# Depthwise convolution of a state-space layer: from ten VectorE taps and six TensorE taps behind a gated recurrence to sixteen taps in 32x32 TensorE tiles that begin inside it

## The chip, the cores and the metric

One NeuronCore of a Trainium2 chip runs the whole program. The metric is the device time of one execution in microseconds (us), the median of several. PE is TensorE, DVE is VectorE, ACT is ScalarE, POOL is GpSimd, SP is SyncE, which here only issues DMAs. DVE, ACT, POOL and SP take their instructions strictly in the order of the program, so a wait at the head of a queue holds everything behind it.

## The reference

The input x has 32 sequences (batches) of 128 time steps with 128 features. The program computes a two-layer model; only its start is touched here:

- a gated recurrence over the 128 time steps, all 32 batches at once: `z = sigmoid(x W_z + h U_z + v_z)`, `r = sigmoid(x W_r + h U_r + v_r)`, `hh = tanh(x W + (r*h) U + v)`, `h = (1-z) h + z hh`. The states of all steps are its output G;
- a state-space layer on G: `zxbcdt = G @ W_in` gives a gate z (256 columns), xBC (384 channels) and dt (8 heads). xBC goes through a causal depthwise convolution of 16 taps along time with a bias, then `silu`. Of its 384 channels 256 are xs (8 heads of 32), 64 are B and 64 are C. The scan `h = h*exp(dt*A) + dt*x*B`, `y = h*C` runs over time for each batch and head; then `y + D*xs`, times `silu(z)`, a root-mean-square norm, `@ W_out`, `y/sqrt(1+y*y)`, `@ W_nl`, and the residual sums.

Behind it follow a local attention, a mixture of experts, two LSTMs, an attention with relative bias and a second mixture. The change doesn't touch those.

## The kernel before

**Order of the work.** Every engine has one hand-written program. `weave(...)` runs several Python generators side by side, one turn (`yield`) each in rotation, and so fixes the order of an engine's queue; semaphores (`inc`, `at`) do the rest. The stages that matter are: the load of x; the recurrence `gru_*` with `mprep_*` (preparation of the state-space weights) woven in; then `mdt_*` (dt and the decay exponents), two workers `mamba_*(wk)` and `conv_*`, all woven; then `cprep_*` (the preparation of the next attention) behind worker 0, while worker 1 ends.

**The recurrence.** Helper `mmh` multiplies a 128x128 weight by a 128x32 state as four matmuls into four column tiles of 32 output rows; a fp32 matmul shows as two LDWEIGHTS and two MATMUL records. A step is: matmuls `gzh` x (U_r, U_z), `tanh` into `gth` on ACT, `grh` and `gq` on DVE, matmul `grh` x U, matmuls `gq` x `gn` for the next step, `tanh` into `ghh`, `gzh` on DVE, and again. PE has a hole while ACT and DVE make `grh` (the first hole) and another while they make `ghh` and `gzh` (the second). Between them go the input projections of later steps (`gru_inputs_pe`, records `X,gw`) in the first hole, and dummy bf16 matmuls that keep PE busy (`gru_warm_pe`, records `identb`). POOL writes each state into G. Banks 0 to 7 of PSUM hold the sums of two groups of 8 steps.

**The convolution.** It starts when the recurrence has ended. The 32 batches are 8 units of 4. For each unit and each of three groups of 128 channels (24 pieces, count n): PE multiplies `win` by G into bank 6; ACT copies it into a padded buffer `XP`; PE adds up the first `NT = 6` taps in bank 7 with diagonal matrices `tap` (128x128 by 512 columns); ACT takes them out with the bias (`B,cb`); DVE adds the other ten taps, each one `scalar_tensor_tensor` of 128x512 (records `work<-work,cw`); ACT and DVE make `silu` from a `tanh` (`conv_act`, `conv_dve`). The C channels are moved to partitions 0 to 63 (the 64x512 records of DVE).

**The scan.** Each worker takes every second unit, 4 units in all, and in each unit one batch after the other (n = 0 to 15). Per batch: ACT makes the decays E (8 heads, records `catt<-tri,catt`), PE sums them with `low` into B1 and B2 (two matmuls of 512 columns), ACT takes `Exp`; PE makes the gate, B^T C and the transposes of xs (`cross`); DVE makes `cbm`, `xdt` (L1007), the product `E*cbm` (L1012); PE makes y in `B0` (D*xs by diagonal `dg`, initial state by `h0T`, 64 records of 128x32 for the heads); DVE finishes y (L1020, L1023, L1024) and the gate. At a unit's end come the norm, transposes, `wout`, a square root and a `reciprocal` of 128x512 (L1040), `wnl`, the sum into X on DVE and X+G on POOL (L1054). Worker 1 starts 14 turns behind worker 0 (`MAMBA_UNIT_TURNS`, 22 against 8).

Of the kernel before, what the change touches and what calls it, by code (L numbers as in the profile page):

```python
# [138 lines left out]
NT = 6  # L139
COND2_LAG = 22  # L140
MAMBA_DT_TURNS = 6
MAMBA_UNIT_TURNS = ((8, 1, 1, 1), (22, 1, 1, 1))
# [20 lines left out]
class Kernel:  # L163
    def __init__(self, nc, ctx, I, out):
# [7 lines left out]
        with nc.sbuf_tensor("spare", [128, 3072], F32) as self.spare:  # L172
            pass
# [43 lines left out]
    def tensor(self, e):  # L217
        self.load_pe(e)
        weave(self.gru_pe(e), self.mprep_pe(e))
        weave((self.mdt_pe(e), 2), chain(self.mamba_pe(e, 0), self.cprep_pe(e)), self.mamba_pe(e, 1), self.conv_pe(e))  # L220
        weave(self.cond2_pe(e, 0), self.cond2_pe(e, 1))
        self.mix_pe(e, 0)
        self.attn_pe(e)
        self.mix_pe(e, 1)

    def scalar(self, e):
        self.load_act(e)
        weave(self.gru_act(e), self.mprep_act(e))
        weave((self.mdt_act(e), 2), chain(self.mamba_act(e, 0), self.cprep_act(e)), self.mamba_act(e, 1), self.conv_act(e))
# [6 lines left out]
    def vector(self, e):  # L236
        self.load_dve(e)
        weave(self.gru_dve(e), self.mprep_dve(e))
        weave((self.mdt_dve(e), 2), chain(self.mamba_dve(e, 0), self.cprep_dve(e)), self.mamba_dve(e, 1), self.conv_dve(e))
# [5 lines left out]
    def gpsimd(self, e):  # L245
        self.constants_pool(e)
        weave(self.gru_pool(e))
        weave(self.conv_pool(e), self.mamba_pool(e, 0), self.mamba_pool(e, 1))
# [127 lines left out]
    def gru_banks(self, t):  # L376


        x = 4 * (t // 8 % 2) + 2 * (t % 2)
        return self.bank[x], self.bank[x + 1]  # L380

    def gru_parts(self, g, odd):

        BR, BZ = self.gru_banks(8 * g + odd)
        return [P.rearrange("p (s b) -> p s b", s=4) for P in (BR[:, 0:128], BR[:, 128:256], BZ[:, 0:128])]

    def gru_condition_pe(self, e, g, odd):

        BR, BZ = self.gru_banks(8 * g + odd)
        mm(e, BR[:, 0:256].rearrange("p (g s b) -> p g s b", g=2, s=4), self.ident[:],  # L390
           bc(self.gV[:, 1:3, :], 2, 4), True, False)
        mm(e, self.gru_parts(g, odd)[2], self.ident[:], bc(self.gV[:, 0, :], 1, 4), True, False)

    def gru_inputs_pe(self, e, g, odd):

        at = self.at
        xq = self.X[:, :, 8 * g + odd:8 * g + 8:2]
        if g < 2:
            self.gru_condition_pe(e, g, odd)
        yield  # L400
        for P, w, bank in zip(self.gru_parts(g, odd), (1, 2, 0), "RRZ"):
            if g >= 2:
                e.wait_ge(*at("gru.c", g, odd, bank))
            mm(e, P.rearrange("p s b -> p b s"), self.gw[:, w, :], xq, False, False)
            yield

    def gru_pe(self, e):


        at, inc, gw = self.at, self.inc, self.gw  # L410
        e.wait_ge(*at("gru.w", "w"))
# [8 lines left out]
        for _ in self.gru_inputs_pe(e, 0, 0):  # L420
            pass
        for t in range(T):
            g = t // 8
            BR, BZ = self.gru_banks(t)
            o = t % 8 // 2 * 32
            e.wait_ge(*at("gru.k", t - 1))
            mmh(e, BR, o, gw[:, 4, :], self.gzh[:]).then_inc(*inc("gru.r", t))
            mmh(e, BZ, o, gw[:, 3, :], self.gzh[:]).then_inc(*inc("gru.z", t))
            if t == 0:
                for _ in self.gru_inputs_pe(e, 0, 1):  # L430
                    pass
            if t % 8 == 0 and t + 8 < T:
                ahead = chain(self.gru_inputs_pe(e, g + 1, 0), self.gru_inputs_pe(e, g + 1, 1))
            next(ahead, None)
            if t % 4 == 0:
                self.gru_warm_pe(e, t, 3)
            e.wait_ge(*at("gru.rh", t))
            mmh(e, BR, o + 128, gw[:, 5, :], self.grh[:]).then_inc(*inc("gru.u", t))
            if t + 1 < T:
                NR, NZ = self.gru_banks(t + 1)  # L440
                o = (t + 1) % 8 // 2 * 32
                e.wait_ge(*at("gru.q", t))
                mmh(e, NR, o, self.gn[:, 1, :], self.gq[:])
# [2123 lines left out]
```

## Time and profile before

| | |
|---|---|
| time, median of 3 runs (lowest, highest) | 2271.31 us (2267.38, 2275.32) |
| the profiled execution: its time, its span | 2269.55 us, 2267.7 us |
| mean granted TensorE clock | 0.951 of full speed |
| busy share of the span | PE 89%, DVE 75%, ACT 44%, POOL 20% |
| the recurrence, from the first `gzh` to the last | 27.6 to 250.1 us |
| state space, to worker 0's and to worker 1's last X+G | 250.2 to 658.4 and to 697.1 us |

Times in the rows are us from the span's start unless they are marked ns. In a group of instructions stand the line and engine, the operation, what it writes and reads, the shape and the count; then the busy time, the mean duration of one in ns, and the idle time of the engine just before with what ended it. Lines 85, 103, 107 and 112 are those of helpers (matmul, activation, scalar_tensor_tensor, tensor_scalar), so groups are told apart by tiles. A matmul's end is modelled and holds the way through the array; matmuls of one engine overlap in the records.

### The profile page before, as it was taken

To read this page: it belongs to the slowest core of one execution; us is meant where nothing else is said; L and a number is where in the kernel's file an instruction comes from. 1 tells how busy PE (TensorE), PEld (TensorE's weight loads), DVE (VectorE), ACT (ScalarE), POOL (GpSimd) and SP (SyncE) were. 2 spreads that over 40 slices of the span, in tenths; PEclk is the share of its full clock that TensorE was granted. 3 is DMA by queue.
4 is the path that set the end of the run, shared out by engine and by line. 5 is a ranking of instruction groups with operands and counts; after the bars stand their busy time and mean duration, and the time that the engine had idled before them with its cause. 6 is when DMAs were issued, how large, how long until landed. Compare 5 with 4: busy or idle time off the path is not lost.

```text
span 2267.7 us, 62486 instructions
## 1 busy us (share of the span) xinstructions
PE 2011.8 (89%) x25711; PEld 1278.0 (56%) x25787; DVE 1698.1 (75%) x3792; ACT 1008.1 (44%) x2835; POOL 459.9 (20%) x794
## 2 busy tenths in 40 slices
PE   7888888998886898898799999985999789999998
PEld 5555534444453444343576677763666556677776
DVE  3443489999965888777888888844999668888887
ACT  2333245666553221221555555542544445555555
POOL 2211000000000434336012222243432111121200
PEclk8999699999978999999999999996999999999999
DMA  2000000000010000000311111106553211111111
GB/s 61 3 4 4 2 1 1 1 1 1 1 38 15 0 1 1 1 1 1 112 48 44 44 44 44 39 4 130 107 108 73 65 40 44 39 44 44 44 57 38
DMA packets 76038, 76.61 MB, mean 34 GB/s; under 512 B 15756, under 2 KB 57060, under 8 KB 74180
## 3 DMA queue, kind: packets, MB, share of 16 engines
q1 hardware_dynamic: 71848, 70.11, 12.3%
q8 instruction: 203, 3.33, 0.6%
q10 hardware_dynamic: 3904, 2.49, 0.4%
q14 instruction: 83, 0.68, 0.1%
HBM read 60.09 MB, written 11.82 MB: 32 GB/s over the span
## 4 chain that ended last, share of the span: by engine, by line
PE 47%; DVE 30%; ACT 9%; issue 8%; DMA 1%; POOL 1%; ACTq 1%; SPq 1%; another core or an unknown queue 1%; DVEq 0%; POOLq 0%
PE B L85 46%; DVE work L107 6%; DVE work L2117 4%; DVE hr L2081 3%; DVE work L2125 3%; ACT work L103 2%; ACT hr L103 2%; ACT ltc L103 2%; DVE work L1496 1%; ACT catt L103 1%; DVE gzh L107 1%; ACT ghh L103 1%; DVE work L1040 1%; ACTq L2404 1%; DVE grh L107 1%
## 5 line engine op out<-in xcount | busy, mean ns | idle before, releaser
L85 PE MATMUL B<-gr,wres 128*128 128x512 f32 x1248 | 354.5, 412 | 16.4 <-DVE work L2125 10.1
L103 ACT ACTIVATE work<-B 128x512 f32<-128x512 f32 (+7 forms) x468 | 240.1, 529 | 145.4 <-PE B L85 90.2
L2167 POOL COPY G<-lh 128x32 f32<-128x32 f32 x256 | 148.2, 579 | 680.0 <-DVE lh L107 680.0
L85 PE MATMUL B<-work 128*128 128x128 bf16 (+3 forms) x1408 | 260.3, 312 | 28.0 <-ACT work L103 7.0
L85 PEld LDWEIGHTS B<-gr,wres 128*128 128x128 f32 x1248 | 215.1, 189 | 83.7 <-DVE work L2125 27.4
L103 ACT ACTIVATE hr<-work 128x512 fp32r<-128x512 f32 x272 | 173.0, 636 | 147.0 <-DVE work L2125 77.5
L85 PEld LDWEIGHTS B<-work 128*128 128x128 bf16 (+2 forms) x1408 | 141.4, 127 | 139.1 <-issue 79.9
L2081 DVE TENSOR_TENSOR hr<-work,hr 128x512 fp32r<-128x512 f32 x272 | 186.5, 686 | 8.1 <-ACT hr L103 6.6
L2117 DVE TENSOR_TENSOR work<-work 128x512 f32<-128x512 f32 x256 | 178.9, 699 | 16.1 <-ACT work L103 8.9
L107 DVE SCALAR_TENSOR_TENSOR work<-work,cw 128x512 f32<-128x512 f32 x240 | 179.2, 747 | 5.9
L85 PE MATMUL B<-hr,wres 128*128 128x512 f32 x624 | 178.0, 394 | 1.0 <-DVE hr L2081 1.0
L103 ACT ACTIVATE lth<-B 128x96 f32<-128x96 f32 (+1 forms) x512 | 86.8, 222 | 187.2 <-PE B L85 187.1
L85 PEld LDWEIGHTS B<-lh,lw 128*32 128x32 f32 x8128 | 88.8, 112 | 112.5 <-issue 58.6
L85 PE MATMUL B<-lh,lw 128*32 128x32 f32 x8128 | 117.0, 199 | 24.5 <-DVE lh L107 23.2
L107 DVE SCALAR_TENSOR_TENSOR work<-B,ckc,work 128x512 f32<-128x512 f32 x160 | 116.7, 742 | 27.1 <-ACT work L103 17.7
L103 ACT ACTIVATE catt<-catt 128x512 f32<-128x512 f32 (+3 forms) x141 | 81.8, 594 | 119.6 <-DVE catt L2417 89.4
L85 PEld LDWEIGHTS B<-hr,wres 128*128 128x128 f32 x624 | 117.2, 188 | 28.2 <-DVE hr L2081 1.9
L1496 DVE TENSOR_TENSOR work<-B,work 128x512 f32<-128x512 f32 x160 | 106.7, 681 | 32.2 <-remote 31.6
L107 DVE SCALAR_TENSOR_TENSOR lh<-lth,ltc 128x32 f32<-128x32 f32 x256 | 49.4, 193 | 106.6 <-ACT ltc L103 106.6
L1533 POOL TENSOR_TENSOR work<-work 128x512 f32<-128x512 f32 x64 | 82.2, 1284 | 209.7 <-DVE work L1496 115.5
L85 PE MATMUL B<-gr,hr 128*128 128x512 f32 x384 | 114.1, 434 | 10.0 <-DVE gr L1435 7.0
L85 PE MATMUL B<-X,lw 128*128 128x128 f32 x512 | 122.0, 323 | 0.0
(262 smaller groups left out, 3777.8 us busy)
## 6 DMA issues: line engine op xcount, KB each, us to landing
work<-wdr SPq DMA_DIRECT2D x128, 256.0 KB, 3.1
scr<-catt SPq DMA_DIRECT2D x144, 64.0 KB, 2.8
work<-scr SPq DMA_DIRECT2D x16, 384.0 KB
work<-scr SPq DMA_DIRECT2D x16, 192.0 KB
catt<-in_L_ffn_ew SPq DMA_DIRECT2D x24, 128.0 KB, 2.2
work<-scr SPq DMA_DIRECT2D x16, 128.0 KB
out<-work SPq DMA_DIRECT2D x32, 64.0 KB, 2.2
work<-in_x ACTq DMA_DIRECT2D x2, 512.0 KB, 5.3
```

Of the source, the lines that this page charges most:

```text
L85: return e.matmul(out, lhsT, rhs, start=start, stop=stop, skip_group_check=True)
L103: return e.activation(out, in_, func, bias=bias, scale=scale)
L107: return e.scalar_tensor_tensor(out=out, in0=a, scalar=s, in1=b, op0=op0, op1=op1)
L1040: e.reciprocal(m["tm"][:], m["tm"][:]).then_inc(*inc(me, "tr", i))
L1496: e.tensor_tensor(four(pr[n % 6]), four(B[:]), KP[:, c, :, j:j + 128], ALU.mult).then_inc(*inc(dve, "v", i, c, j))
L1533: e.tensor_tensor(av, u0, u1, ALU.add).then_inc(*inc(f"cd{wk}.pool", i, c))
L2081: e.tensor_tensor(hr[1][:], self.hh[j % 4], hr[0][:].bitcast(F32), ALU.subtract).then_inc(*self.inc("m.dve", "h", li, j))
L2117: e.tensor_tensor(src, self.sg[i], self.Wb[n % 4], ALU.mult).then_inc(*inc("m.dve", "pu", li, k))
L2125: h = stt(e, self.hh[m], U, 0.5, src, ALU.mult, ALU.mult) if li else e.tensor_tensor(self.hh[m], U, src, ALU.mult)
L2167: e.tensor_copy(self.G[:, :, t], self.lh[:, t % 4, :]).then_inc(*inc("l.pool", "h", li, t))
L2404: e.dma_start(self.aQ[u % 4][48 + q:49 + q, :, :], self.anT[16 * q:16 * q + 16, :]).then_inc(*self.dma("at.max", u))
```

## The change

- **Recurrence.** Its PSUM use shrinks to banks 0, 1 (reset and candidate, odd and even steps) and 2 (update gate). Input projections move from the first hole to the second (`gru_ahead_pe`), the gate's as one matmul of 256 columns for 8 steps. ACT's refresh of the sums (`gru_condition_act`) moves ahead of the `ghh` tanh, and PE waits for it before the `gq` matmuls of steps 0 to 2 of a group of 8. Dummy matmuls stay in the first 32 steps only, fewer of them.
- **Convolution.** All 16 taps go to PE, over chunks of 32 time steps and all 32 batches (4 chunks x 3 channel groups = 12 rounds n). A round has 16 tap pieces, each of 16 matmuls of 32x32 weights by 256 columns: row group i is 32 channels, column tile j 8 batches, output bank 4+i; and 4 input pieces (128x128 by 256 columns, bank 3). From step 32 one piece is issued in each step's first hole; what is left (`conv_rest_pe`) runs behind the recurrence and ahead of the scan. ACT copies inputs and takes results out; from round 4 on DVE takes out two of the four banks. POOL makes `tap` and copies the 15-step halos.
- **Scan.** Results lie by slots, `cv[32*j+channel, slot, k, t]`: a slot holds 4 batches, 8 apart. `silu` moves into the workers (three `tanh` and three DVE products per unit), `dg` and the per-batch `xdt` go; in their place `turn` transposes a unit's xs in two halves into bank 6+wk and `turned` makes `xdt` and `xD` from each half (four DVE operations of 128x512 per unit), and one more DVE sum of 128x256 per batch adds `xD`.
- **Loads.** The conv bias comes as 48 DMAs of 32 values instead of 3, D as 1 instead of 8; PE waits for them at step 4 of the recurrence (before, at step 122).

```diff
-NT = 6
+CONV_STEP = 32
+CHUNK = 32
...
-        weave((self.mdt_pe(e), 2), chain(self.mamba_pe(e, 0), self.cprep_pe(e)), self.mamba_pe(e, 1), self.conv_pe(e))
+        self.conv_rest_pe(e)
+        weave(chain(self.mamba_pe(e, 0), self.cprep_pe(e)), self.mamba_pe(e, 1))
...
+            elif t >= CONV_STEP:
+                next(conv, None)
+            elif t % 2:
+                self.gru_warm_pe(e, t, 1)
             e.wait_ge(*at("gru.rh", t))
-            mmh(e, BR, o + 128, gw[:, 5, :], self.grh[:]).then_inc(*inc("gru.u", t))
+            mmh(e, U, 0, gw[:, 5, :], self.grh[:]).then_inc(*inc("gru.u", t))
...
                 e.wait_ge(*at("gru.q", t))
-                mmh(e, NR, o, self.gn[:, 1, :], self.gq[:])
-                mmh(e, NZ, o, self.gn[:, 0, :], self.gq[:])
-            self.gru_warm_pe(e, t, 1)
+                if 8 <= t < T - 8 and t % 8 < 3:
+                    e.wait_ge(*at("gru.c", t // 8 + 1, t % 8))
+                mmh(e, NR, 0, self.gn[:, 1, :], self.gq[:])
+                mmh(e, NZ, 0, self.gn[:, 0, :], self.gq[:])
+            self.gru_ahead_pe(e, t)
...
+    def conv_taps_pe(self, e, n, k):
+
+        at, c = self.at, n % 3
+        if k == 0:
+            e.wait_ge(*at("conv.x", n, 3))
+            if n:
+                self.conv_evicted(e, n - 1)
...
+        for j in range(4):
+            for i in range(4):
+                r = slice(32 * i, 32 * i + 32)
+                last = mm(e, self.bank[4 + i][32 * j:32 * j + 32, 0:256], self.tap[r, 16 * c + k, :],
+                          self.XP[c][r, 8 * j:8 * j + 8, k:k + CHUNK], k == 0, k == 15)
...
+        for n in range(12):
+            k = 0
+            for x in range(20):
+                if x in (12, 14, 16, 18):
+                    if n == 11:
+                        continue
+                    self.conv_input_pe(e, n + 1, (x - 12) // 2)
+                else:
+                    self.conv_taps_pe(e, n, k)
+                    k += 1
+                yield
+            for _ in range(4):
+                yield
...
+        def turned(i, h):
+            hs, o = slice(4 * h, 4 * h + 4), self.slot(wk, i)
+            e.wait_ge(*at(pe, "xt", i, h))
+            if i and h == 0:
+                e.wait_ge(*at(pe, "y", 4 * i - 1))
+            e.tensor_tensor(m["xdt"][:, hs], B3, bc(self.dth[:, o:NB:8, hs].rearrange("p j h -> p h j"), 3, 32), ALU.mult)
+            e.tensor_tensor(m["xD"][:, hs].rearrange("p h j q -> p h (j q)"), B3.rearrange("p h j q -> p h (j q)"),
+                            bc(self.drow[:, hs], 2, 128), ALU.mult).then_inc(*inc(me, "xd", i, h))
```

## Rows read from the trace of the kernel before

**Rows 1.** X+G on POOL, the end of a unit, in order of time
```profile
392.74 1.76 POOL L1054 TENSOR_TENSOR X<-X,G 128x512 f32<-128x512 f32 x1 [141.58 <-DVE X L107]
...
487.51 1.78 POOL L1054 TENSOR_TENSOR X<-X,G 128x512 f32<-128x512 f32 x1 [43.42 <-DVE X L107]
...
582.30 1.78 POOL L1054 TENSOR_TENSOR X<-X,G 128x512 f32<-128x512 f32 x1 [43.42 <-DVE X L107]
...
658.41 1.26 POOL L1054 TENSOR_TENSOR X<-X,G 128x512 f32<-128x512 f32 x1 [23.82 <-DVE X L107]
```
**Rows 2.** Busy time by stretch: three with convolution, one without, recurrence's end
```profile
core 0: us, PE busy (x) PEld busy (x) DVE busy (x) ACT busy (x) POOL busy (x), PEclk, DMA share, GB/s
...
392.74:582.30 189.56, 170.22 (x1496) 86.80 (x1483) 176.67 (x289) 117.04 (x281) 7.08 (x5) 0.98 0.00 1
...
636.00:657.60 21.60, 16.91 (x236) 9.21 (x226) 14.70 (x29) 15.86 (x35) 0.00 (x0) 0.90 0.01 2
...
582.30:658.41 76.11, 63.15 (x687) 34.44 (x686) 64.91 (x111) 48.86 (x118) 3.04 (x2) 0.88 0.01 2
...
250.20:278.90 28.70, 25.10 (x83) 18.33 (x84) 12.91 (x32) 2.61 (x6) 0.55 (x4) 0.62 0.00 1
```
**Rows 3.** Groups of DVE by form, 392.74 to 582.30 us
```profile
L107 DVE SCALAR_TENSOR_TENSOR work<-work,cw 128x512 f32<-128x512 f32 x120 | 89.4, 745 | 2.8
...
L107 DVE SCALAR_TENSOR_TENSOR work<-work 64x512 f32<-64x512 f32 x9 | 10.0, 1113 | 0.3
...
L1007 DVE TENSOR_TENSOR work<-B,catt 128x256 f32<-128x256 f32 x16 | 6.6, 414 | 0.0
...
L107 DVE SCALAR_TENSOR_TENSOR work<-work 128x512 f32<-128x512 f32 x8 | 5.5, 690 | 8.5 <-ACT work L103 8.5
...
L1044 DVE TENSOR_TENSOR work<-work,B 128x512 f32<-128x512 f32 x4 | 2.7, 681 | 0.0
```
**Rows 4.** Groups of ACT and PE by form, 392.74 to 582.30 us
```profile
L103 ACT ACTIVATE work<-B 128x512 f32<-128x512 f32 x24 | 14.1, 596 | 16.6 <-PE B L875 12.9 <-PE B L85 3.7
L103 ACT ACTIVATE work<-work 128x512 f32<-128x512 f32 x16 | 10.1, 630 | 39.7 <-DVE work L107 28.3 <-DVE work L1040 11.4
L103 ACT ACTIVATE work<-B,cb 128x512 f32<-128x512 f32 x12 | 8.2, 682 | 1.9 <-PE B L85 1.9
...
L103 ACT ACTIVATE catt<-B 128x256 f32<-128x256 f32 x16 | 6.1, 380 | 7.3 <-PE B L85 7.2
...
L85 PE MATMUL B<-work 128*128 128x512 f32 x144 | 65.4, 595 | 2.3 <-ACT work L103 2.3
...
L85 PE MATMUL B<-G,win 128*128 128x512 f32 x24 | 13.0, 625 | 0.0
```
**Rows 5.** Instructions in order of time, one step of the recurrence (start, duration)
```profile
150.60 0.33 PE L85 MATMUL B<-gzh,gw 128*32 128x32 f32 x16
...
150.87 0.30 PEld L85 LDWEIGHTS B<-X,gw 128*128 128x128 f32 x2
150.87 0.49 PE L85 MATMUL B<-X,gw 128*128 128x128 f32 x2
...
151.48 0.16 PEld L85 LDWEIGHTS B<-grh,gw 128*32 128x32 f32 x8 [0.32 <-DVE grh L107]
...
151.59 0.33 PE L85 MATMUL B<-gq,gn 128*32 128x32 f32 x16
151.82 0.20 ACT L103 ACTIVATE ghh<-B 128x32 f32<-128x32 f32 x1 [0.59 <-PE B L85]
151.85 0.10 PEld L85 LDWEIGHTS B<-identb 128*128 128x128 bf16 x1
...
152.30 0.16 PEld L85 LDWEIGHTS B<-gzh,gw 128*32 128x32 f32 x8 [0.35 <-DVE gzh L107]
```
**Rows 6.** PE in order of time, three places: taps, three column tiles, 64 small tiles
```profile
427.81 2.85 PE L85 MATMUL B<-work 128*128 128x512 f32 x6 [1.18 <-ACT work L103]
...
745.44 1.06 PE L85 MATMUL B<-work,selh 128*32 128x512 f32 x6
...
651.51 0.76 PE L85 MATMUL B<-work,catt 128*32 128x32 f32 x64
```
**Rows 7.** SP's DMA issues in order of time, and PE behind the recurrence
```profile
17.69 1.37 SPq L572 DMA_DIRECT2D cb<-in_L_attn_conv_b  x3
...
250.99 13.82 PE L85 MATMUL B<-win,G 128*128 128x8 f32 x64 [0.80 <-POOL G L112]
```

More of the change, by code:

```diff
@@ L429, in gru_pe @@
             if t == 0:
[L430 to L436, printed above, removed]
+                self.gru_condition_pe(e, 0, 1)
+                self.gru_inputs_pe(e, 0, 1, 0)
+                self.gru_inputs_pe(e, 0, 1, 1)
+            elif t >= CONV_STEP:
+                next(conv, None)
+            elif t % 2:
+                self.gru_warm_pe(e, t, 1)
@@ L622, in mdt_pe @@
         last.then_inc(*self.inc("mdt.pe", "x"))
-        for _ in range(12):
-            yield
+        for _ in self.conv_rest:
+            pass
         e.wait_ge(*at("mdt.dve", "a"))
@@ L730, in conv_act @@
-        taps_out(n - 1)
-        tanh(n - 2)
-        for _ in range(4):
-            yield
-        tanh(n - 1)
+        yield
+        for j in range(4):
+            self.conv_input_act(e, 0, j)
+            yield
+            yield
+        for n in range(12):
+            for _ in range(11 + (n > 0)):
+                yield
+            for j in range(4):
+                yield
+                if n < 11:
+                    self.conv_input_act(e, n + 1, j)
+                yield
+            for i in range(4):
+                if i not in self.conv_out_dve(n):
+                    e.wait_ge(*at("conv.w", n))
+                    out, B, b = self.conv_place(n, i)
+                    act(e, out, B, ACT.Identity, bias=b).then_inc(*inc("conv.act", n))
+                yield
@@ L924, in squares, with tanh @@
                 *inc(me, "ss", n))
-        for _ in range(MAMBA_DT_TURNS):
+        def tanh(i, c):
+            if c:
+                e.wait_ge(*at(dve, "silu", i, c - 1))
+            elif i:
+                e.wait_ge(*at(dve, "silu", i - 1, 2))
+            else:
+                self.conv_evicted(e, 11)
+            act(e, m["th"], self.cv[:, self.slot(wk, i), 4 * c:4 * c + 4, :].rearrange("p k t -> p (k t)"), ACT.Tanh,
+                scale=0.5).then_inc(*inc(me, "th", i, c))
+        for _ in range(MAMBA_LAG * wk):
             yield
@@ L933, in mamba_act @@
         yield
+        tanh(0, 2)
         gate(0)
@@ L947, in mamba_act @@
                 yield
+                if j < 3 and i < 3:
+                    tanh(i + 1, j)
                 yield
```

482 lines of the change are left out of this document (253 added, 229 removed).

## The prediction

> **What bounds the kernel now.** I read the page first for the stage's place, then the ends of the units, then the busy time by stretch, then the groups by form of each engine, and last single steps in order of time. The ends of worker 0's units [rows 1] show a rhythm: 392.74, 487.51, 582.30, so 94.8 us for a pair of units (one of each worker), and 76.1 us for the last pair, whose later part has no convolution beside it. In the two full pairs DVE is busy 176.67 of 189.56 us, 93% [rows 2]; of that 89.4 + 10.0 + 5.5 = 104.9 us are tap and `silu` operations of the convolution [rows 3]. DVE bounds this stage, and the convolution is 59% of DVE. PE is at 90% there too, so moving work to PE is only a gain where PE has holes or where its form is cheaper. The recurrence in front is a chain: a step takes 1.70 us (150.60 to 152.30 [rows 5]), DVE and ACT are mostly waiting, and PE has a first hole from the end of the `gzh` matmuls to 151.48 and a second from the end of `gq` to 152.30. From 636.0 to 657.6 both workers run without the convolution: ACT is busy 73%, DVE 68%, PE 78%, at a granted clock of 0.90 [rows 2]. No engine is full there; the chains of the workers set the pace. That is the state in which the change puts the whole scan.
>
> **The price of a tap piece.** A round has 16 pieces and there are 12 rounds, so 192 pieces of 16 fp32 matmuls, 32 MATMUL records each. Streaming: six tap records of 512 columns take 2.85 us, the last of them 0.59 and the first load 0.11, so 0.43 us for each (2.85 - 0.59 - 0.11, by 5) [rows 4, 6]; 256 columns take half, 0.215. Three column tiles side by side, six records of 512 columns with different moving data, take 1.06 us, where one after the other they would need some 2.6; two passes of three, 0.43 each, plus the way through the array [rows 6]. So column tiles run together at full rate, first pass of all and then second. Issue: 64 records of small tiles take 0.76 us, (0.76 - 0.20) / 64 = 9 ns each, so 32 need 0.28 us and hide under the stream [rows 6]. If all 16 tiles run together a piece costs 2 x 0.215 = 0.43 us. No row of this trace has two row groups at once. If only four tiles run together it is 8 x 0.215 / 2 = 0.86 us with the passes of one four overlapping the next, or 1.72 without; if each matmul must end before the next, 3.4 to 6.9 us. I take 0.43: the three column tiles are the nearest row, and they share rows of the array, which tiles of different row groups do not. The Trainium skill (TensorE: Matmul & The Clock Gate, Part 3) gives 10.6 times for 16 such tiles, not 16; no row here shows it. By it a piece would be an estimated 6.9 / 10.6 = 0.65 us, and the sum below 30 to 40 us longer.
>
> **Sum, part 1: the recurrence.** Of the pieces, 96 slots lie in steps 32 to 127: 8 for the first inputs (4 filled), then 24 a round, four of them empty. That puts 62 tap pieces and 18 inputs inside, and 130 tap pieces and 30 inputs behind.
> - First hole: `X,gw` starts at 150.87, the next load at 151.48 [rows 5]. A piece that starts at 150.87 issues its last tile some 0.12 us behind its first, streams to 150.87 + 0.12 + 0.43 = 151.42, and the change of tile shape costs about 0.1 (`gzh` issue ends near 150.76, `X,gw` starts at 150.87): 151.52, 0.04 us late.
> - Second hole: the moved `X,gw` starts at 151.85 in place of `identb`, its second record 0.22 later; it streams to 152.18, plus 0.1: just in time for 152.30. The 256-column one of each 8 steps ends 0.2 later: 0.02 per step. In three of 8 steps ACT's refresh (128x256, 0.38 [rows 4]) ends near 151.62 and holds the `gq` matmuls from 151.59 to 151.68; with `X,gw` behind them that is 0.07 late, 0.03 per step.
> - 96 x (0.04 + 0.02 + 0.03) = 9 us. ACT's copies (0.38) fit between `ghh`'s end at 152.02 and the next `gth`, some 0.6 us.
> - Loads: an issue on SP takes 1.37 / 3 = 0.46 us [rows 7]; 48 + 1 instead of 3 + 8 make 38 more, 18 us, so the last lands near 39 us instead of 21, and PE's queue wants it at step 4, near 36.5: +2.5 us, with all of the recurrence's matmuls behind that wait.
> - Together +11 us (bounds 0, if the holes swallow all, and +25, if each step slips 0.25): the last `gzh` at 261 instead of 250.
>
> **Part 2: what runs behind it.** The 64 dt records took 13.82 us at a clock of 0.62 over that stretch [rows 2, 7]. At full clock a 128-column load takes 0.11 (0.30 for two overlapping, [rows 5]), so 6.9 us; with pieces keeping PE busy to the end I take full clock: 269. Then 130 x 0.43 = 56, 30 inputs x (0.11 + 0.43 + two changes of shape 0.2) = 22, and at each of 9 round ends PE stands until the four banks are out. ACT takes two at 0.4 each (between 0.38 of the 256 and 0.68 of the 512 columns [rows 4]), DVE two beside it, with the way through the array and two semaphores 1.1 us, 10 in all. End: 269 + 88 = 357. The rule that tiling speeds the matmuls but not the way out of PSUM (the Trainium skill, TensorEngine Tiling, Performance Considerations) speaks against this change; those 10 us are its price here, already in the sum. The POOL halos and DVE's dt chain lie beside this.
>
> **Part 3: the scan.** Per pair of units DVE has 88.3 us; the convolution's 52.4 go, so 35.9. `xdt` goes (8 x 0.414 = 3.3); in come 6 products of 0.69, 8 operations of `turned` at 0.68, 8 sums at 0.42 [rows 3]: 4.1 + 5.4 + 3.4, gives 45.5. ACT has 58.5; the convolution's 12 + 12 + 12 operations in two pairs (7.2 + 8.2 + 7.6) are 11.5 a pair; 6 `tanh` of 0.63 come back: 50.8 [rows 4]. PE has 85.1, less (65.4 + 13.0) / 2 = 39.2 [rows 4]: 46. At the shares of the stretch without convolution the pair would take 50.8 / 0.73 = 69, 45.5 / 0.68 = 67 or 46 / 0.78 = 59 us. I take 67: ACT and DVE both say so. Bounds: 59 and the 76.1 of the last pair. Four pairs 268; before the first, some 11 us (three `tanh`, the decays at 2.4, three products, two transposes and `turned`). Worker 0's last X+G at 357 + 11 + 268 = 636 instead of 658.4. Behind it `cprep` and worker 1's end stay as they are: it lags 14 turns as before.
>
> The sum is 22 us less than the profiled 2269.55: 2247.5; the median is 1.8 above that execution, so 2249.
>
> **Rivals.**
> - *Pieces do not run back to back.* All pieces of a round add into the same banks, so each could wait for the one before: 0.43 + 0.12 + some 0.1 = 0.65. Behind the recurrence +0.22 x 130 = 28, in the holes +5: 2282. Against it: the tap records of before add into one bank without a gap [rows 6]. This lands where the 10.6 of the skill would.
> - *Only four tiles at a time* (slower than before). 0.86 a piece: 56 us behind, and in 62 steps the hole overflows by 0.43, 27 us: 2332. It decides from 0.54 us per piece: 22 us over 192 pieces is 0.115 on top of 0.43. For it: the trace shows four tiles at most; against it: nothing that limits them.
> - *Less than that.* Two passes of a matmul back to back on one tile, or row groups that exclude each other: 1.7 to 3.4 a piece, 2495 to 2820.
> - *The scan without filler goes slower.* With DVE and ACT each at two thirds, a granted clock that falls, and one more operation behind y, a pair of 80 us: +52, 2301. For it: from 582.30 to 658.41 the clock was 0.88, from 392.74 to 582.30 0.98 [rows 2].
>
> **How the numbers follow.** As summed: 0.65, with its own range 2205 to 2299 (pair 59 to 76, recurrence 0 to +25). Not back to back 0.10, four tiles 0.11, less 0.08, slow scan 0.06. The range 2205 to 2340 leaves out the 0.08 and the ends of the others. A difference of 0.3%, 7 us, is about what a measurement of this kernel can tell. Of the first case four fifths are faster by more than that, 0.52, and 0.02 of the slow-piece and slow-scan cases with a good scan or good pieces beside them; 0.10 is within it; the rest, 0.36, slower.
>
> **What would show it.** The step of the recurrence from step 32 on: 1.79 us is right, 1.70 means the holes are free, over 2.0 means pieces are dear. The time of 16 pieces behind the recurrence: 6.9 us is right. From the last `gzh` to the first decay: 96 us. The distance of worker 0's X+G: 67 us, with DVE near 68% and ACT near 76%. The prediction falls if a piece costs over 0.54 or a pair over 73 us.

## The result and the profile after

The change made the kernel slower: 2396.75 us (median of 4 runs, 2389.16 to 2407.62) against 2271.23 us for the kernel before on the same chips, a ratio of 1.0556 with an interval of 1.0508 to 1.0604. The forecast was 2249 us, faster; the time also lies above its range. Of the after kernel's page, the head, the PE line and PE's instruction queue (packets, MB, share):

```profile
span 2398.3 us, 73929 instructions
...
PE 2082.1 (87%) x31509; PEld 1326.5 (55%) x31509; DVE 1547.7 (65%) x3573; ACT 1010.1 (42%) x2854; POOL 466.9 (19%) x806
...
q8 instruction: 248, 4.06, 0.7%
```

The same two lines of the page of before, which the prediction had not used:

```profile
PE 2011.8 (89%) x25711; PEld 1278.0 (56%) x25787; DVE 1698.1 (75%) x3792; ACT 1008.1 (44%) x2835; POOL 459.9 (20%) x794
...
q8 instruction: 203, 3.33, 0.6%
```

Busy time by stretch of the after kernel (columns as in [rows 2]): first 32 steps of the recurrence, the other 96, the dt records, what runs behind them, two pairs of units:

```profile
25.60:107.90 82.30, 64.67 (x1409) 38.79 (x1409) 25.57 (x134) 19.40 (x110) 20.98 (x57) 0.59 0.04 3
107.90:308.90 201.00, 170.26 (x5912) 101.17 (x5912) 64.94 (x381) 64.77 (x347) 31.72 (x98) 0.81 0.02 4
308.90:324.60 15.70, 14.79 (x66) 14.15 (x66) 1.20 (x4) 0.23 (x2) 0.32 (x1) 0.50 0.00 1
324.60:466.60 142.00, 115.52 (x4221) 69.16 (x4220) 17.77 (x42) 20.91 (x54) 3.60 (x6) 0.95 0.02 4
549.39:706.54 157.15, 126.43 (x1338) 66.83 (x1337) 99.20 (x181) 104.65 (x256) 5.81 (x5) 0.78 0.01 1
```

X+G on POOL, worker 0's four units, which answer to [rows 1]:

```profile
549.39 1.64 POOL L1152 TENSOR_TENSOR X<-X,G 128x512 f32<-128x512 f32 x1 [133.53 <-DVE X L107]
...
628.02 1.64 POOL L1152 TENSOR_TENSOR X<-X,G 128x512 f32<-128x512 f32 x1 [30.05 <-DVE X L107]
...
706.54 1.65 POOL L1152 TENSOR_TENSOR X<-X,G 128x512 f32<-128x512 f32 x1 [30.05 <-DVE X L107]
...
779.12 1.26 POOL L1152 TENSOR_TENSOR X<-X,G 128x512 f32<-128x512 f32 x1 [24.13 <-DVE X L107]
```

Where the time went, stretch by stretch (the boundaries are read off the two traces; `gzh` by its operation on DVE, and the 27.6 and 25.6 us ahead of the first are left out):

| stretch | before, us (clock) | after, us (clock) |
|---|---|---|
| first `gzh` to that of step 32 | 60.0 (0.91) | 82.2 (0.59) |
| steps 32 to 127 | 162.5 (0.97) | 201.0 (0.81) |
| last `gzh` to the first decay | 28.8 (0.62) | 157.7 (0.91) |
| first decay to worker 0's last X+G | 379.5 | 312.5 |
| from there to worker 1's | 38.7 | 41.7 |
| the rest | 1570.6 | 1577.4 |

The scan did what it was changed for, 67 us less, but the recurrence and the stretch behind it take 190 us more. Against the prediction's own sum, worker 0's last X+G is 143 us late (779 in place of 636): 48 us in the recurrence, 61 between it and the scan, 34 in the scan.

**A piece, read closely.** PE in order of time, two steps of the recurrence in the after kernel (start, duration):

```profile
201.49 0.76 PE L85 MATMUL B<-work 32*32 32x256 f32 x32
...
202.18 0.27 PE L85 MATMUL B<-grh,gw 128*32 128x32 f32 x8
...
223.61 1.17 PE L85 MATMUL B<-work 32*32 32x256 f32 x32
224.71 0.34 PE L85 MATMUL B<-grh,gw 128*32 128x32 f32 x8
```

The first is a step at full clock: the `grh` matmuls follow 0.69 us behind the start of the piece, where [rows 5] had 0.61 for the hole. The second is the same at the lower of the clock's two levels (1.2 in place of 2.4 GHz): 1.10 us. Behind the recurrence, PE and then its weight loads:

```profile
309.81 13.82 PE L85 MATMUL B<-win,G 128*128 128x8 f32 x64 [1.24 <-POOL G L112]
...
378.28 0.70 PE L85 MATMUL B<-G,win 128*128 128x256 f32 x2
378.91 0.71 PE L85 MATMUL B<-work 32*32 32x256 f32 x32
379.56 0.70 PE L85 MATMUL B<-G,win 128*128 128x256 f32 x2
...
382.86 3.39 PE L85 MATMUL B<-work 32*32 32x256 f32 x159 [1.96 <-DVE work L112]
```

```profile
382.83 2.95 PEld L85 LDWEIGHTS B<-work 32*32 32x32 f32 x160 [2.41 <-issue]
386.50 2.29 PEld L85 LDWEIGHTS B<-work 32*32 32x32 f32 x128 [0.73 <-issue]
390.25 1.66 PEld L85 LDWEIGHTS B<-work 32*32 32x32 f32 x96 [1.46 <-issue]
```

Five pieces run without a break in 3.39 us. Less the last one's own 0.71 that is 0.67 us a piece, where the prediction took 0.43; the granted clock from 382.8 to 390.3 us is 1.00. Then PE stands with "issue" as the reason, that is, with nothing that the profile shows; the next run starts at 386.50 and holds exactly 128 loads and 128 matmuls, 256 instructions, four pieces; the one after starts 3.75 us later. So four pieces cost 3.7 us, 0.92 each. And the instruction queue fits: PE has 63018 instructions and 248 packets after, 51498 and 203 before; 11520 more instructions by 45 more packets are 256 per packet (the trace of before lacks 76 of PE's matmul records, so this holds to within a few). The gap falls where a new packet of instructions is needed. That was the first theory to test; the low clock was the second.

### The profile page after: what moved, and what is told of

Read it like the earlier page. It is cut to its first block, busy times and chain, and to the rows that moved or that the text cites. A ratio compares the mean times of both kernels' runs of the same rounds, so it can differ in the third digit from the quotient of the medians.

```text
span 2398.3 us, 73929 instructions
## 1 busy us (share of the span) xinstructions
PE 2082.1 (87%) x31509; PEld 1326.5 (55%) x31509; DVE 1547.7 (65%) x3573; ACT 1010.1 (42%) x2854; POOL 466.9 (19%) x806
## 4 chain that ended last, share of the span: by engine, by line
PE 56%; DVE 22%; ACT 9%; issue 8%; SPq 2%; DMA 1%; ACTq 1%; POOL 1%; DVEq 0%; POOLq 0%
PE B L85 54%; DVE work L2215 4%; DVE work L107 3%; DVE hr L2179 3%; DVE work L2223 2%; ACT catt L103 2%; ACT hr L103 2%; ACT ltc L103 2%; SPq L625 1%; ACT work L103 1%; ACTq L2502 1%; DVE work L1594 1%; DVE lth L107 1%; DVE lpq L107 1%; DVE lh L107 1%
## 5 line engine op out<-in xcount | busy, mean ns | idle before, releaser
L103 ACT ACTIVATE work<-B 128x512 f32<-128x512 f32 (+6 forms) x480 | 236.9, 509 | 229.1 <-PE B L85 187.4
L85 PE MATMUL B<-work 32*32 32x256 f32 (+2 forms) x7328 | 288.6, 394 | 32.7 <-DVE work L112 12.5
L85 PEld LDWEIGHTS B<-work 32*32 32x32 f32 (+2 forms) x7328 | 174.0, 109 | 129.0 <-issue 79.8
L85 PE MATMUL B<-catt,low 128*128 128x512 f32 x128 | 96.4, 899 | 38.0 <-ACT catt L103 30.9
```

What stands on the lines that cost most here:

```text
L85: return e.matmul(out, lhsT, rhs, start=start, stop=stop, skip_group_check=True)
L103: return e.activation(out, in_, func, bias=bias, scale=scale)
```

## The experiments

All are compared with the kernel before (2269 to 2271 us), and each edit is to the kernel after unless another is named.

**Bias loads.** The 48 loads of the conv bias get a semaphore of their own, which the first take-out waits for.

```diff
-                pairs.append((self.cb[...], col(I["L0_attn_conv_b"][...])))
+                late.append((self.cb[...], col(I["L0_attn_conv_b"][...])))
...
+                    if n + i == 0:
+                        e.wait_ge(*at("ld.cvb"))
```

> The 48 bias loads get a semaphore of their own that only the first take-out of the convolution waits for. If step 4 of the recurrence (7.95 us instead of 1.70) waits for the last load of the state-space weights, that step falls to some 1.8 to 2.4 us and steps 0 to 31 get 5 to 6 us shorter (82.3 to about 76.5). Rival: the step is long because of the eight small transposes woven in there; then it stays near 8 us.

Measured: 2391.08 us, ratio 1.0529 (1.0469 to 1.0589). Step 4 takes 2.69 us in place of 7.95 and the first 32 steps 74.6 in place of 82.2. In the after kernel the wait is plain in SP's and PE's own order of time:

```profile
14.69 23.68 SPq L625 DMA_DIRECT2D cb<-in_L_attn_conv_b  x47
```

```profile
39.71 0.65 PE L85 MATMUL B<-ident,h 128*32 128x128 f32 x8 [4.85 <-DMA cb<-in_L_attn_conv_b]
```

So the load wait is real: 5.3 us in its own step and 7.6 over the first 32, where the prediction said 2.5. The 5.7 us in the whole time (2396.75 to 2391.08) are no more than what the runs of one kernel differ by.

**Dummies back in the recurrence.** Three in the first hole of each of the first 32 steps; from step 32 one that adds zeros in the second hole.

```diff
-            elif t % 2:
-                self.gru_warm_pe(e, t, 1)
+            else:
+                self.gru_warm_pe(e, t, 3)
...
+            elif t + 1 < T:
+                mm(e, self.bank[(t + 1) % 2][...], self.identb[:], bc(self.zb[:], 1, 3), False, False)
```

> Puts dummy bf16 matmuls back: three in the first hole of each of the first 32 steps, and one of 384 columns (adding zeros to the next step's bank) in the second hole of every later step. Theory clock: the recurrence is slow because the granted clock falls to half when PE does less between the steps; with dummies steps 32 to 127 go from 201 us to some 165 to 175 at a granted clock over 0.95 (0.81 now), steps 0 to 31 from 82 to about 68, total 2340 to 2360. Theory overflow: the pieces themselves don't fit the hole; then steps 32 to 127 stay at 200 us or get longer by the dummies' 0.16 us each (215).

Measured: 2379.94 us, ratio 1.0475 (1.0429 to 1.0521). Its stretches (first 32 steps, the rest, behind):

```profile
25.90:97.80 71.90, 61.27 (x1487) 35.23 (x1487) 27.63 (x133) 19.08 (x109) 21.27 (x57) 0.95 0.05 4
97.80:294.90 197.10, 171.62 (x6007) 98.34 (x6006) 65.68 (x381) 64.95 (x347) 31.85 (x98) 0.97 0.02 4
```

The clock theory is right for the first 32 steps (0.59 to 0.95, 10 us gained). The other 96 take 197.1 us even at 0.97, where it said 165 to 175. There, at full clock, the weight loads of PE show the same gap as behind the recurrence:

```profile
120.41 0.30 PEld L85 LDWEIGHTS B<-X,gw 128*128 128x128 f32 x2
...
121.58 0.10 PEld L85 LDWEIGHTS B<-zb,identb 128*128 128x128 bf16 x1 [0.88 <-issue]
...
125.58 0.11 PEld L85 LDWEIGHTS B<-grh,gw 128*32 128x32 f32 x1 [0.86 <-issue]
...
129.59 0.17 PEld L85 LDWEIGHTS B<-work 32*32 32x32 f32 x12 [1.02 <-issue]
```

From 121.58 to 125.58 and from there to 129.59 it is 128 loads each. In all, 16 such gaps of 0.45 to 1.20 us stand in these 96 steps, most of them one or two times 128 loads behind the one before (to within missing records), 13 us together; a part of that is the ordinary wait of a step.

The 197.1 us hold a price of the dummies too, which the last fp32 runs below let one read: without pieces and at a clock of 1.00 the same 96 steps take 173.0 us with a dummy in every second hole and 164.2 where the holes with a moved projection have none. If the dummies cost the same beside pieces, the steps of this run would take an estimated 188 us without that price. So of the after kernel's 201.0 the low clock is an estimated 13 us. Four runs in which steps 32 to 127 are the same code, but for the order of the 16 tiles in the last, agree in direction: 201.0, 202.2, 196.0 and 197.2 us (after kernel, bias loads, fewer pieces, order of the tiles) at clocks of 0.81, 0.78, 0.86 and 0.83.

**All pieces behind.** `CONV_STEP = 128`, dummies in both holes of every step.

```diff
-CONV_STEP = 32
+CONV_STEP = 128
```

> All convolution pieces behind the recurrence, which keeps the new bank layout, the moved input projections and dummies in both holes of every step. Theory clock: recurrence 1.70 to 1.78 us a step, 225 to 235 us with the load wait, granted clock near 1.0; the pieces cost 0.65 to 0.8 us each behind it, so 192 pieces and 48 inputs take about 200 us instead of 140: total within 15 us of the changed kernel. Theory layout: the recurrence is slow by its banks, the refresh and the moved projections; then it stays over 2.0 us a step without pieces.

Measured: 2424.70 us, ratio 1.0677 (1.0614 to 1.0741).

```profile
98.30:271.30 173.00, 168.45 (x4275) 95.71 (x4275) 64.61 (x381) 55.16 (x317) 30.02 (x95) 1.00 0.01 4
271.30:497.20 225.90, 186.44 (x6306) 117.11 (x6306) 18.69 (x46) 32.56 (x83) 5.72 (x10) 0.92 0.02 4
```

Without pieces and at full clock the recurrence takes 173.0 us here, 10.5 more than before's 162.5. Most of that is not the layout but the dummies in the second holes: the version with all pieces behind and fewer of them (the first of the two under "What the measurements point to") has the same layout, the moved projections and the refresh, and takes 164.2 us:

```profile
92.00:256.20 164.20, 158.39 (x4215) 93.33 (x4214) 64.58 (x380) 55.16 (x317) 30.06 (x95) 1.00 0.01 4
```

So the moved projections and the refresh cost 1.7 us and the dummies 8.8. The pieces inside cost 24 us at full clock (197.1 less 173.0, both with dummies), and with the low clock 37 in the after kernel (201.0 less 164.2). They are not free, but behind the recurrence the same 62 pieces and 18 inputs cost 68 us (225.9 less 157.7), so beginning them inside is right. What was expected for the stretch behind, about 200 us, was missed, and so was a total within 15 us of the after kernel (28 more).

**Fewer pieces.** Taps 4 to 11 of rounds 4 to 11 left out, 64 pieces that all lie behind the recurrence (not the reference's convolution).

```diff
             for i in range(4):
+                if n >= 4 and 4 <= k < 12:
+                    continue
```

> Leaves out taps 4 to 11 in rounds 4 to 11, all of which run behind the recurrence: 64 tap pieces are gone (the result is not the reference's). If a piece behind the recurrence costs 0.43 us as forecast, 27 us go; at 0.65, the pitch of the pieces in the trace, 42 us; at 0.8, with the idle stretches of PE in which it waits for nothing shown, 52 us.

Measured: 2331.05 us, ratio 1.0265 (1.0199 to 1.0331). From the last `gzh` to the first decay 103.8 us in place of 157.7: 54 us for 64 pieces, 0.84 us each, inputs and round ends unchanged. The gaps are in it: between 0.67 without and 0.92 with one for every four pieces. (The whole time fell by 66 us; 5 of the other 12 lie in steps 32 to 127, which the edit does not touch.)

**Narrow pieces.** Taps 1 to 14 read and write 32 of 256 columns, with the same number of instructions (not the reference's convolution). It tells streaming from instructions.

```diff
+                m = 8 if k in (0, 15) else 1
-                last = mm(e, self.bank[4 + i][32 * j:32 * j + 32, 0:256], self.tap[...], self.XP[c][r, 8 * j:8 * j + 8, k:k + CHUNK], ...)
+                last = mm(e, self.bank[4 + i][32 * j:32 * j + 32, 0:32 * m], self.tap[...], self.XP[c][r, 8 * j:8 * j + m, k:k + CHUNK], ...)
```

> Taps 1 to 14 of every round take 32 columns (one batch of eight) instead of 256; the number of instructions stays, the result is not the reference's. Theory instruction supply: PE stands every 256 of its instructions because a block of 16 KB of them has to arrive, and a block takes at least 3.4 us; then a piece behind the recurrence (64 instructions, a quarter block) still costs about 0.8 us and the stretch from the last gzh to the first decay shrinks by less than 20 us of 158, and the steps of the recurrence with pieces stay near 2.0 us. Theory stream: a piece falls to some 0.35 us; that stretch falls by 50 us or more, and the steps fall to 1.75.

Measured: 2414.53 us, ratio 1.0641 (1.0565 to 1.0718), slower, not faster, with an eighth of the columns in 14 of 16 taps. Weight loads behind the recurrence, and its stretches (steps 32 to 127, behind):

```profile
398.53 1.96 PEld L85 LDWEIGHTS B<-work 32*32 32x32 f32 x160 [2.76 <-issue]
402.31 1.41 PEld L85 LDWEIGHTS B<-work 32*32 32x32 f32 x128 [1.82 <-issue]
405.78 1.08 PEld L85 LDWEIGHTS B<-work 32*32 32x32 f32 x96 [2.06 <-issue]
```

```profile
108.83:320.36 211.53, 181.34 (x5912) 124.03 (x5912) 64.61 (x381) 65.74 (x347) 31.76 (x98) 0.51 0.02 4
320.36:489.08 168.72, 112.67 (x4286) 75.68 (x4286) 19.02 (x46) 21.30 (x55) 3.93 (x7) 0.51 0.01 3
```

The four pieces are issued in 1.41 us instead of 2.29, and PE stands 1.82 us before them instead of 0.73: the starts of the runs are 3.78 and 3.47 us apart, as before (3.67 and 3.75). The streaming does not set the pace of a run of pieces; the arrival of 256 instructions does. With less streamed by PE the granted clock was 0.51 in both stretches, in place of 0.81 and 0.91, and the recurrence was slower still (211.5 us); behind it 168.7 us passed in place of 157.7, so this run does not separate the two by its stretches, only by its packets.

**Narrow pieces with dummies.** The same edit and the dummies of the second experiment, so that the clock does not hide the answer in the recurrence.

> The narrow pieces of the run before (middle taps over 32 of 256 columns, same number of instructions, so not the reference's result) together with the dummy matmuls of the run with dummies: three in the first hole of every step, one adding zeros in the second hole of every step from 32 on. The pieces then carry almost no streaming. Theory A (PE's instructions come in blocks of 256, each at least 3.4 us after the one before, and the pieces bring a step over what fits): steps 32 to 127 stay near the 197 us of full pieces with dummies, 188 to 200, at a granted clock over 0.9, and the stretch from the last gzh to the first decay stays near 155 to 160. Rival B (the pieces' streaming overflows the hole by 0.1 to 0.2 us): steps 32 to 127 fall to the 173 us of the run with all pieces behind the recurrence, at most 178.

```profile
97.50:299.50 202.00, 175.21 (x6007) 111.57 (x6006) 65.11 (x381) 64.87 (x347) 31.56 (x98) 0.78 0.02 4
299.50:467.70 168.20, 111.53 (x4286) 75.30 (x4286) 18.98 (x46) 21.25 (x55) 3.92 (x7) 0.52 0.01 3
```

Measured: 2401.06 us, ratio 1.0575 (1.0544 to 1.0606). Steps 32 to 127 take 202.0 us, near the 197.1 of full pieces and far from 173 to 178; but the clock was 0.78, not over 0.9 as expected, so the last few us of the comparison are not clean. Behind the recurrence it was 168.2 us at a clock of 0.52, not the 155 to 160 expected. It speaks against the streaming overflow and does not by itself prove the supply.

**Half the pieces, twice as wide.** Chunks of 64 steps, 6 rounds of 512 columns, all behind the recurrence, no dummies added.

```diff
-CONV_STEP = 32
-CHUNK = 32
+CONV_STEP = 128
+CHUNK = 64
...
-                last = mm(e, self.bank[4 + i][32 * j:32 * j + 32, 0:256], self.tap[r, 16 * c + k, :],
+                last = mm(e, self.bank[4 + i][32 * j:32 * j + 32, 0:512], self.tap[r, 16 * c + k, :],
```

> Chunks of 64 time steps instead of 32, six rounds, 512 columns a matmul, all behind the recurrence: the same columns in half the matmuls (96 tap pieces, 24 inputs). Theory supply: the pieces are now long enough for the blocks to arrive in time; a piece takes 1.08 us (two passes of 0.43 and the 0.2 between pieces), and from the last gzh to the first decay pass about 155 us against 226 with 32-step chunks all behind. Theory stream (cost goes by columns, 0.84 per 256): 210 us or more.

Measured: 2419.76 us, ratio 1.0664 (1.0609 to 1.0720). PE in one round:

```profile
376.54 14.47 PE L85 MATMUL B<-work 32*32 32x512 f32 x384 [3.39 <-DVE work L112]
390.94 1.12 PE L85 MATMUL B<-G,win 128*128 128x512 f32 x2
```

Twelve pieces of 512 columns take 14.4 us with no gap between the matmuls, 1.20 each for the work of two pieces: four of them take longer than 256 instructions need to arrive. The clock was 0.50 from 378 to 380 us and 1.00 from 382 on; at full clock a piece between two inputs takes 1.06 us. Less the stream of 0.86 that is 0.20, and 0.67 less 0.43 is 0.24: a part for each piece that hardly changed between 256 and 512 columns. The stretch behind the recurrence is 168.2 us, 58 less than the 225.9 with all pieces behind at 256 columns (155 was expected; PE stands 3.4 us at each round end and the first inputs are not overlapped). But the recurrence without pieces or dummies ran at a clock of 0.52 and took 217.1 us for steps 32 to 127, 44 more than the 173.0 with dummies at 1.00. That ate the gain.

**Dummies in the scan.** Six bf16 matmuls ahead of each pair of decay sums.

```diff
+            for _ in range(6):
+                mm(e, B1[:, 0:384]..., self.identb[:], bc(self.identb[:], 1, 3), True, True)
             e.wait_ge(*at(a, "E", n))
```

> Six dummy bf16 matmuls of 384 columns ahead of each batch's decay sums, where PE stands waiting for ACT's decays. Theory clock: a pair of units takes 78.6 us because PE's clock is at half for part of it (granted 0.76); with dummies it rises over 0.9 and the pair falls to 68 to 72 us, 25 to 40 us in all. Theory chain: the workers' chains set the pace at either clock; the pair stays within 2 us of 78.6 or gets longer by the dummies' 1 us per batch.

Measured: 2381.37 us, ratio 1.0495 (1.0440 to 1.0550). The groups of the decay sums in two pairs of units, after kernel first, then with dummies:

```profile
L85 PE MATMUL B<-catt,low 128*128 128x512 f32 x66 | 48.2, 874 | 19.6 <-ACT catt L103 17.1 <-DVE catt L107 2.5
```

```profile
L85 PE MATMUL B<-catt,low 128*128 128x512 f32 x64 | 33.7, 653 | 8.9 <-ACT catt L103 8.9
```

The clock goes from 0.78 to 0.90 and a decay-sum matmul from 874 to 653 ns. Worker 0's first two pairs take 73.8 us each on average (544.85 to 692.42) in place of 78.6, the third 70.5 in place of 72.6, and from the first decay to worker 0's last X+G it is 298.0 us in place of 312.5. So 14.5 of the 34 us by which the scan missed its term (279) are given back, with the price of the dummies still in it; 25 to 40 were expected.

**Order of the 16 tiles.** Row groups outer, column tiles inner.

```diff
-        for j in range(4):
-            for i in range(4):
+        for i in range(4):
+            for j in range(4):
```

> Swaps the two loops of a piece: the four column tiles of a row group come one after the other, then the next row group. If the 0.65 us between two pieces (256 columns need 0.43) come from the order in which row groups and banks are taken, the pitch inside an uninterrupted run of pieces falls to 0.45 to 0.55 and 10 to 25 us go; if it is the start of a new set of weights behind the last tile of the old, it stays at 0.65 and the time within 6 us.

Measured: 2395.89 us, ratio 1.0559 (1.0517 to 1.0601); 158.3 us behind the recurrence against 157.7. The order does not matter, and what the 0.2 us between two pieces are stays open.

**What the measurements point to.** Chunks of 64, late bias loads, dummies in the recurrence where a step has room, and in the scan; once with all pieces behind, once with the first two rounds inside from step 64.

```diff
-CONV_STEP = 128
+CONV_STEP = 64
```

> The best version that the measurements so far point to, all pieces behind the recurrence: chunks of 64 steps (half the pieces, each over 512 columns), late bias loads, three dummies in each first hole, one in the second hole of the first 32 steps and of the steps without a moved projection, six dummies ahead of the decay sums. From the parts: recurrence 72 + 173 less 0 to 6, 245; last gzh to first decay 168; scan 4 pairs at 72 and 11, 299; against before's 87.6 + 162.5 + 28.8 + 379.5 that is 54 us more at worker 0's last X+G: near 2325 to 2340, slower than before. If the recurrence without pieces but with these few dummies falls to a low clock, up to 2370.

> The same, with the 512-column pieces of the first two rounds in the recurrence's first holes from step 64 on (ACT alone takes them out), zero-adding dummies in the second holes without a moved projection. A piece of 512 columns takes about 0.95 to 1.3 us and a first hole 0.61, so a step with one slips 0.5 to 0.8 us: 32 pieces x 0.65 = 21 us more inside against two rounds, some 45 to 50 us, less behind: 2300 to 2320. If a piece must run between steps at its full price, inside and behind cost the same, and the run equals the one with all behind within 10 us. Either way the theory says it stays slower than before.

Measured: 2344.22 us, ratio 1.0325 (1.0295 to 1.0355), and 2309.46 us, ratio 1.0172 (1.0132 to 1.0212), the first 4 us above what was expected, the second within it. In the second, steps 64 to 127 take 2.16 us each on average, and the stretch behind is 103.4 us. With fp32 pieces no version here beats the kernel before.

**bf16 pieces.** The taps and the padded inputs as bf16, so a matmul is one pass: 32 instructions a piece and not 64, and less streaming (products of inputs rounded to bf16). The expectations call that half; it is less: a piece of 512 columns on its own shows 0.44 us in bf16 and 1.14 in fp32. First in the last version, then in the run with dummies and chunks of 32.

```diff
-        self.tap = ar(128, 48, 32)
-        self.XP = [ar(128, NB, CHUNK + 15) for _ in range(3)]
+        self.tap = ar(128, 48, 32, dt=BF16)
+        self.XP = [ar(128, NB, CHUNK + 16, dt=BF16) for _ in range(3)]
```

> The version with 64-step chunks and two rounds inside the recurrence, with taps and padded inputs held as bf16, not fp32 (so the convolution's products are rounded to bf16 inputs). A bf16 matmul needs one pass, not two: a piece is 32 instructions of PE, not 64, and streams 512 columns once. Theory (a piece costs what its passes stream and what its instructions take to arrive, 256 in at least 3.4 us, 0.43 us a piece): inside, pieces fit the first hole, so steps 64 to 127 fall from about 2.19 to 1.70 to 1.80 us, 25 us less; behind, 64 pieces at 0.45 in place of 1.06 are 39 to 43 us less, so last gzh to first decay 103 to about 62. Together 2309 less 65: 2240 to 2250, faster than the kernel before. Rival (the 16 tiles' own turn-round or the clock sets the price): less than half of that, 2275 or more.

> The run with dummies and chunks of 32 steps, with taps and padded inputs as bf16 and nothing else changed: half the instructions and half the streaming in each of the 192 pieces (products of inputs rounded to bf16). Theory (instruction supply, 0.43 us for 32 instructions): steps 32 to 127 from 197 to 173 to 178 us; last gzh to first decay from 155 to 155 less 130 x 0.41 = 102; all together 2300 to 2310. Rival (a price by tile or by piece, at least the 0.65 of an uninterrupted fp32 piece): last gzh to first decay 130 or more, 2335 or more.

The version with everything took 2249.61 us (10 runs; before 2271.30), ratio 0.9907 (0.9880 to 0.9933): 0.9% faster than the kernel before, and as expected (2240 to 2250). Its stretches (first 32 steps, the other 96, behind, three pairs of units):

```profile
26.10:90.50 64.40, 59.41 (x1487) 34.43 (x1487) 27.54 (x133) 19.01 (x109) 21.20 (x57) 1.00 0.05 4
90.50:266.70 176.20, 159.12 (x4686) 92.83 (x4686) 64.63 (x381) 66.27 (x337) 30.10 (x95) 0.89 0.02 4
266.70:335.30 68.60, 53.13 (x990) 31.79 (x991) 17.27 (x38) 13.43 (x24) 1.93 (x4) 0.73 0.01 2
416.60:634.60 218.00, 184.17 (x2130) 100.60 (x2128) 144.45 (x260) 149.91 (x368) 8.56 (x7) 0.90 0.01 2
```

Against the same version in fp32, steps 32 to 127 are 16 us shorter (192.3 to 176.2) and the stretch behind 35 (103.4 to 68.6), both somewhat less than expected (from step 64 on a step takes 1.90 us, not 1.70 to 1.80), at a lower clock (0.97 to 0.89 in the first, 0.88 to 0.73 in the second).

With bf16 alone, 2342.53 us, ratio 1.0309 (1.0270 to 1.0348), 37 us less than its fp32 twin (2379.94) and short of the 2300 to 2310 of the theory. PE's packets in this run:

```profile
q8 instruction: 225, 3.69, 0.7%
```

and the packets of its fp32 twin:

```profile
q8 instruction: 249, 4.08, 0.8%
```

The first two weight loads of a round in the bf16 run, and its stretches (steps 32 to 127, behind):

```profile
335.37 1.88 PEld L85 LDWEIGHTS B<-work 32*32 32x32 bf16 x137 [3.05 <-issue]
338.86 0.78 PEld L85 LDWEIGHTS B<-work 32*32 32x32 bf16 x55 [1.61 <-issue]
```

```profile
97.40:301.10 203.70, 181.68 (x5015) 108.38 (x5014) 64.58 (x380) 65.47 (x347) 31.51 (x98) 0.67 0.01 4
301.10:423.40 122.30, 88.18 (x2206) 54.19 (x2206) 18.94 (x46) 21.97 (x54) 4.13 (x7) 0.50 0.01 2
```

From a round's start to its first gap 137 loads pass, eight and a half pieces of 16 loads, where fp32 had 160, five pieces of 32; and the next run starts 3.49 us behind the round's start, there 3.67. That is 0.41 us a piece in place of 0.73. The queue has 24 packets fewer than the twin's for 6144 instructions fewer (192 pieces x 32), 256 for each again. So the pace of an uninterrupted run of pieces goes by the instruction, not by the piece or the tile, nor, by the narrow pieces, by the column. (A round of this run has no second run between two gaps, so the comparison is that of the first.) Inside the recurrence the forecast failed: 203.7 us in place of 173 to 178, more than the twin's 197.1. The clock was 0.67 there and 0.50 behind it, where everything between the gaps (inputs, round ends) is slower too. The rival is met by the total (2335 or more) and not by the stretch behind, at least 130 us against 122.3; so the stretches and the total decide nothing here, and the reading rests on the packets and the loads.

## Why the prediction was wrong, by its own steps

- **"I take 0.43."** This is the step that failed. The parts that it argued from hold in the main: 32 x 0.215 us of streaming in 0.67 are some ten tiles at once on average, where before showed four at most, and the 32 loads of a piece are issued in 0.23 us. But the price of an uninterrupted piece is 0.67 us, and with the wait for instructions 0.84 on the average behind the recurrence. 130 x (0.84 - 0.43) = 53 us, most of the 61 lost there. The prediction's bounds asked what tiles may run at once and never what 64 instructions in 0.43 us need to arrive. The 0.67 is what the rival of pieces that do not run back to back had (0.43 and some 0.2 more), and the 1.06 at 512 columns has the same 0.2. The Trainium skill (TensorE: Matmul & The Clock Gate, Part 3) gives the gain of 16 small tiles as 10.6 times, measured with 512 columns. Taken over to 256 columns it makes an estimated 0.65 us, and the trace has 0.67; at its own 512 columns it would be an estimated 32 x 0.43 / 10.6 = 1.30 us, where the trace has 1.06. So the prediction had a price near the right one at hand and put it aside, but the agreement at 256 columns is in part chance.
- **"96 x (0.04 + 0.02 + 0.03) = 9 us."** Measured +38.5 for steps 32 to 127. The moved projections and the refresh are 1.7 of that, less than the 4.8 that the sum had for them (96 x 0.05). The pieces are 24 at full clock, where it had 4, and the clock of 0.81 an estimated 13, for which no term stood. In the rows of a step at full clock the hole overflows by only 0.08 us, about 5 us for 62 pieces. Instructions are the rest as far as is known: in the run with dummies a step without a piece has some 83 (PE and its loads), one with a piece 147, and 256 in 3.5 us allow a step of 2.0 us, not 1.70 to 1.80; the packets there were 4.0 us apart. The 16 gaps add up to 13 us at most. What the remaining 6 or more are stays open.
- **The load wait, "+2.5 us".** Right in kind, 6.3 us in size (7.95 less before's 1.69): 47 issues took 23.68 us, 0.50 each and not 0.46, and the steps ahead of step 4 began earlier than taken.
- **The clock, taken as full.** In the first 32 steps it fell from 0.91 to 0.59, 10 us that no term held (the dummies were fewer, not gone). "With pieces keeping PE busy to the end I take full clock" for the dt records failed outright: 13.82 us, the same as before, at 0.50, 7 us more than the term.
- **"I take 67" a pair.** Measured 78.6, the term 34 us short over the scan. The slow-scan rival, 80 us a pair with a falling clock, described it. Its mechanism is shown for 14.5 us by the dummies, which have a price of their own in that number; for the other 20 the chain of the two workers is the likely place, which stays unproved. ACT's and DVE's busy times came out near the estimate (52.3 and 49.6 a pair against 50.8 and 45.5), so the operation count was right (DVE's 4 us short) and the share at which they would run was not. PE's did not: 63.2 us of busy time a pair against 46 (126.43 for two pairs), at a granted clock of 0.78.
- **The rivals.** Four tiles at a time was priced at 0.86 us a piece, +56 us behind and +27 inside. Measured are +53 and, at full clock, 24: nearly its numbers, by another mechanism. That the time lies 65 us above its 2332 (70 by the profiled executions) comes from what was priced alone or not at all: 34 in the scan, 10 behind worker 0's last X+G, 18 in the first 32 steps (10 of them the clock), an estimated 13 of low clock in the other 96 and 7 in the dt records, less some 12 by which pieces and layout cost less than it said.
- **The sum.** 48 (recurrence) + 61 (behind) + 34 (scan) = 143 us at worker 0's last X+G, less the forecast gain of 22, and 10 us more in what follows it (worker 1's end and the rest; the cause of these was not looked for): 131 us, which is the difference of the two spans, 2398.3 less 2267.7.

## What to carry to other kernels

Price a stream of small matmuls by its instructions as well as by its columns: a 32x32 fp32 matmul is four instructions of PE, and here 256 instructions took about 3.5 us to arrive, so fewer and wider tiles, or one pass in place of two, come before any packing of holes. Dummies have a price as well: one beside a moved projection cost 0.16 us a step here (1.89 against 1.73 in the two runs with all pieces behind and a clock of 1.00). When work is moved to PE's holes or dummies are taken out, read the granted clock of each stretch and carry the lower level as a case of its own in every term, together with the others. A count of the instruction queue's packets on the page, before and after, tells in a minute whether an edit brings many instructions.

## What the runs showed of the hardware

- PE's instruction queue moves one packet for each 256 instructions of PE (11520 more by 45 packets; 6144 fewer with bf16 by 24). In runs of small matmuls the gaps are 3.5 to 3.8 us apart, at granted clocks from 1.00 to 0.50 (4.0 inside the recurrence), and PE stands until the next 256 instructions start; idle time with "issue" as its reason at steps of exactly 256 instructions is the sign.
- Sixteen 32x32 fp32 tiles of 256 columns overlap, a new set each 0.67 us at full clock; of 512 columns each 1.06 with an input between, and 1.20 on average in a long run that began at a clock of 0.50.
- The same number of PE instructions ran at different granted clocks: narrow pieces at 0.51 and 0.51 (recurrence, behind it) where full ones had 0.81 and 0.91. The recurrence without pieces ran at 1.00 with dummies and at 0.52 without, 173.0 and 164.2 us (more and fewer dummies) against 217.1 us for the same chain.
